# Two-layer macaron block on one core: routing taken further ahead, three PSUM banks in turn for the experts, and the second call's row scatters in twos

## What is computed

```python
x = x + 0.5 * ffn(layernorm(x))          # call 0
x = x + attn(layernorm(x))               # state-space mixer, then a gated FFN
x = x + 0.5 * ffn(layernorm(x))          # call 1

def ffn(x):
    shared = (silu(x @ sw1) * (x @ sw2)) @ sw3
    probs = softmax(x @ rw + rb)                 # 8 experts
    w, idx = top_k(probs, 2); w = w / sum(w)
    routed = sum over the two chosen e of w_e * ((silu(x @ ew1[e]) * (x @ ew2[e])) @ ew3[e])
    return shared + routed
```

## Time and profile before

| | us |
|---|---|
| median of 3 timed runs | 864.18 (860.76 to 873.64) |
| profiled execution | 854.65 |
| its span, first to last instruction | 852.9 |
| PE busy in the span | 658.5 |
| DVE busy | 546.5 |
| POOL busy | 518.7 |
| ACT busy | 413.9 |

### The profile page before, as it was taken

One profiled execution on the slowest core, in us unless ns is written; L12 is line 12 of the kernel. 1 busy time (PEld: TensorE's weight loads), 2 busy tenths in 40 slices (PEclk: granted clock), 3 DMA queues, 4 the chain that ended last, 5 costly groups with the idle time before them and its releaser, 6 DMA issues.

```text
span 852.9 us, 13745 instructions
## 1 busy us (share of the span) xinstructions
PE 658.5 (77%) x3768; PEld 479.3 (56%) x3768; DVE 546.5 (64%) x1730; ACT 413.9 (49%) x713; POOL 518.7 (61%) x656
## 2 busy tenths in 40 slices
PE   2548389888870557989999998989774989889940
PEld 2325257777760225656676765757552568777730
DVE  5545355544545787897999999997452545554528
ACT  1212124444430899997999998652121234444310
POOL 3875573555564675896978879767736305555550
PEclk9987789999995859889999998999978899999975
DMA  9311123222215100000000000000101123222218
GB/s 268 129 50 37 41 70 73 77 75 74 70 43 158 40 0 1 1 2 1 1 2 1 2 14 13 14 19 24 41 14 45 50 45 81 73 73 75 63 46 271
DMA packets 55512, 46.34 MB, mean 54 GB/s; under 512 B 8456, under 2 KB 51053, under 8 KB 55440
## 3 DMA queue, kind: packets, MB, share of 16 engines
q1 hardware_dynamic: 46736, 28.54, 12.6%
q0 software_dynamic: 8704, 16.93, 6.1%
HBM read 25.30 MB, written 21.19 MB: 55 GB/s over the span
## 4 chain that ended last, share of the span: by engine, by line
PE 47%; DVE 15%; issue 12%; another core or an unknown queue 11%; ACT 9%; POOL 3%; DMA 2%; DVEq 0%; POOLq 0%; ACTq 0%; SPq 0%
PE ps_go L2029 5%; PE ps_tr L1631 3%; PE ps_a L1971 3%; PE ps_b L1973 3%; PE ps_go L1981 3%; PE ps_go L1631 2%; DVE x L1516 2%; PE ps_go L1802 2%; PE ps_tr L1819 2%; PE ps_go L1806 2%; PE ps_b L1853 2%; PE ps_go L2018 2%; PE ps_go L1852 2%; POOL ys L710 1%
## 5 line engine op out<-in xcount | busy, mean ns | idle before, releaser
L710 POOL DMA_INDIRECT ys<-arena,dest x144 | 140.9, 978 | 145.1 <-DVE arena L1508 60.3
L694 POOL DMA_INDIRECT xs<-rows,pos x128 | 126.0, 985 | 72.8 <-DVE pos L1428 36.6
L2029 PE MATMUL ps_go<-w_down_e,arena 128*128 x576 | 80.0, 282 | 17.7 <-DVE arena L1508 15.7
L2029 PEld LDWEIGHTS ps_go<-w_down_e,arena 128*128 128x128 f32 x576 | 71.0, 194 | 24.0 <-issue 23.7
L1508 DVE COPY arena<-ps_go 128x256 f32<-128x256 f32 x72 | 30.6, 424 | 63.7 <-remote 40.5
L992 ACT ACTIVATE silu_a<-ps_a 128x512 f32<-128x512 f32 x32 | 19.1, 596 | 87.8 <-PE ps_a L1971 42.6
L1004 ACT ACTIVATE xt_hi<-ps_tr 128x256 fp32r<-128x256 f32 x72 | 27.4, 384 | 67.4 <-PE ps_tr L1992 42.5
L1021 ACT ACTIVATE arena<-ps_go 128x512 f32<-128x512 f32 x72 | 43.1, 598 | 28.5 <-remote 14.3
L1498 DVE TENSOR_TENSOR hid<-silu_a,ps_a 128x512 f32<-128x512 f32 x36 | 24.7, 687 | 41.1 <-ACT silu_a L1012 29.4
L2018 PE MATMUL ps_go<-ident,hid 128*128 128x128 f32 x288 | 44.0, 276 | 5.2 <-ACT arena L1021 5.1
L2018 PEld LDWEIGHTS ps_go<-ident,hid 128*128 128x128 f32 x288 | 35.1, 142 | 17.6 <-issue 7.7
(11 more groups left out here) (359 smaller groups left out, 1996.8 us busy)
## 6 DMA issues: line engine op xcount, KB each, us to landing
arena<-xs SPq DMA_DIRECT2D x144, 65.0 KB
rows<-ys SPq DMA_DIRECT2D x8, 512.0 KB, 4.2
arena<-ys SPq DMA_DIRECT2D x8, 512.0 KB, 7.5
ys<-arena,dest POOLq DMA_INDIRECT x144
x<-in_L_attn_x SPq DMA_DIRECT2D x8, 256.0 KB, 4.5
arena<-in_L_ffn_ew SPq DMA_DIRECT2D x4, 512.0 KB, 6.4
xs<-rows,pos POOLq DMA_INDIRECT x128
out<-x SPq DMA_DIRECT2D x8, 256.0 KB, 4.1
```

The lines of the kernel that those rows point to most:

```text
L694: pool.indirect_dma_start(xs, bass.IndirectOffsetOnAxis(pos[:, n, i:i + 1], 0), rows[:, n * TT + i % TT, :], None).then_inc(scattered, 16)
L710: pool.indirect_dma_start(ys, bass.IndirectOffsetOnAxis(dest[:, i:i + 1], 0), y_out[:, p % YRING, j, :], None, bounds_check=2 * TOK - 1, o ...
L2029: r = pe.matmul(ps_k[:, j * P:(j + 1) * P], hid_t[:, p % 2, at:at + P], w_down_e[:, bass.ds(which[2 * p + j], 1), k, :].rearrange("p a d - ...
```

## The change

Four edits. In call 0 the queues of PE, ScalarE and VectorE are written in another order, so that logits and choices are made two blocks ahead of the shared FFN and the ranks come first in each step. In call 1 the late blocks' routing is spread over more steps, and stands later in the queues. In the experts stage of both calls the banks `ps_k`, `ps_t` and `ps_r` are used in turn for transposes and answers; the wait for an answer's copy stands at the transposes now (`pe_tiles_t`), from the sixth pair on. In call 1, those of the mixer included, each pair of scatters waits until all scatters ahead of it have landed.

```diff
+        ps_turn = (ps_k, ps_t, ps_r)
+        def ps_tiles(p):
+            return ps_turn[(2 * p + 1) % 3][:, 0:2 * P]
+        def ps_answers(p):
+            return ps_turn[(2 * p + 2) % 3][:, 0:2 * P]
...
             pool.wait_ge(pos_ready, turn + 1)
             for i in which:
+                if turn >= NB and i % 2 == 0:
+                    pool.wait_ge(scattered, 16 * (turn * 2 * TT + i))
                 pool.indirect_dma_start(xs, bass.IndirectOffsetOnAxis(pos[:, n, i:i + 1], 0),
...
         def pe_tiles_t(pe, call, p):
             pair = call * NPAIR + p
-            after(pe, lo_ready, pair - 1)
+            if p >= 5:
+                pe.wait_ge(answer_ready, pair - 4)
...
-                r = pe.transpose(ps_tr[:, p % 2, j * P:(j + 1) * P], x_tiles[:, i % XIN, 0:P], ident[:, :])
+                r = pe.transpose(ps_tiles(p)[:, j * P:(j + 1) * P], x_tiles[:, i % XIN, 0:P], ident[:, :])
...
             pe.wait_ge(ht_ready, pair + 1)
-            after(pe, answer_ready, pair)
+            if p + 2 >= NPAIR:
+                pe.wait_ge(answer_ready, pair - 2)
...
             for n in range(1, NB + 2):
+                if n + 1 < NB:
+                    dve_places(dve, own, n + 1)
+                if n + 3 < NB:
+                    dve_norm(dve, n + 3)
                 if n + 2 < NB:
-                    dve_norm(dve, n + 2)
-                if n + 1 < NB:
-                    dve_route(dve, own, n + 1)
+                    dve_route(dve, own, n + 2)
                 if n <= NB:
                     dve_hid(dve, n - 1, 0)
-                if n + 1 < NB:
-                    dve_places(dve, own, n + 1)
-                if n + 2 == NB:
+                    dve_hid(dve, n - 1, 1)
+                if n + 1 == NB:
                     dve_tiles(dve, own, 0)
-                if n <= NB:
-                    dve_hid(dve, n - 1, 1)
...
             for n in range(NB + 1):
-                late = EARLY + n
+                late = EARLY + n - 1
                 if n < NB:
                     pe_up(pe, NB + n, 0)
-                if late < NB:
+                if EARLY <= late - 2 < NB:
+                    pe.wait_ge(rank_read, NB + late - 2)
+                    pe_rank(pe, NB + late - 2)
+                if EARLY <= late - 1 < NB:
+                    pe.wait_ge(logits_read, NB + late - 1)
+                    pe_route_logits(pe, late - 1, ps_r)
+                if n < NB:
+                    pe_up(pe, NB + n, 1)
+                if EARLY <= late < NB:
                     pe.wait_ge(xt_ready, NB + n + 2)
                     pe_route_xt(pe, late, ps_t)
...
```

More of the change, by code:

```diff
@@ L1025, in act_ffn @@
             act_xt(act, 1)
+            act_xt(act, 2)
             act.wait_ge(shared_in, 48)
@@ L1547, in dve_ffn @@
             dve_norm(dve, 2)
+            dve_norm(dve, 3)
+            dve_route(dve, own, 2)
             dve_w_lo(dve, 0)
             for n in range(1, NB + 2):
+                if n + 1 < NB:
+                    dve_places(dve, own, n + 1)
+                if n + 3 < NB:
+                    dve_norm(dve, n + 3)
                 if n + 2 < NB:
-                    dve_norm(dve, n + 2)
-                if n + 1 < NB:
-                    dve_route(dve, own, n + 1)
+                    dve_route(dve, own, n + 2)
                 if n <= NB:
                     dve_hid(dve, n - 1, 0)
-                if n + 1 < NB:
-                    dve_places(dve, own, n + 1)
-                if n + 2 == NB:
+                    dve_hid(dve, n - 1, 1)
+                if n + 1 == NB:
                     dve_tiles(dve, own, 0)
-                if n <= NB:
-                    dve_hid(dve, n - 1, 1)
                 if n >= 2:
@@ L1571, in dve_ffn_again @@
             dve.wait_ge(mixer_done, NB)
-            late = range(EARLY, NB)
-            for n in late:
+            for n in range(EARLY, NB):
                 dve_stats(dve, own, NB + n)
-            for n in late:
-                dve_norm(dve, NB + n)
             for n in range(NB + 1):
+                late = EARLY + n - 1
                 if n < NB:
                     dve_hid(dve, NB + n, 0)
-                if 1 <= n <= NB - EARLY:
-                    dve_places(dve, own, NB + EARLY + n - 1)
+                if EARLY <= late - 2 < NB:
+                    dve_places(dve, own, NB + late - 2)
+                if EARLY <= late - 1 < NB:
+                    dve_route(dve, own, NB + late - 1)
                 if n < NB:
                     dve_hid(dve, NB + n, 1)
+                if n == 0:
+                    for m in range(EARLY, NB):
+                        dve_norm(dve, NB + m)
                 if n:
                     dve_shared(dve, NB + n - 1)
-                if n < NB - EARLY:
-                    dve_route(dve, own, NB + EARLY + n)
-                if n == NB - EARLY:
+                if late - 2 == NB - 1:
                     dve_tiles(dve, own, 1)
@@ L2040, in pe_ffn @@
             pe_rank(pe, 0)
+            pe_logits(pe, 1)
             for n in range(NB + 1):
                 if n + 1 < NB:
-                    pe_logits(pe, n + 1)
+                    pe.wait_ge(rank_read, n + 1)
+                    pe_rank(pe, n + 1)
+                if n == 0:
+                    pe_xt(pe, 2)
+                if n + 2 < NB:
+                    pe_logits(pe, n + 2)
                 if n == 1:
@@ L2059, in pe_ffn @@
                     pe_down(pe, n - 2)
+                if n + 3 < NB:
+                    pe_xt(pe, n + 3)
             pe_down(pe, NB - 1)
@@ L2069, in pe_ffn_again @@
             for n in range(NB + 1):
-                late = EARLY + n
+                late = EARLY + n - 1
                 if n < NB:
                     pe_up(pe, NB + n, 0)
-                if late < NB:
+                if EARLY <= late - 2 < NB:
+                    pe.wait_ge(rank_read, NB + late - 2)
+                    pe_rank(pe, NB + late - 2)
+                if EARLY <= late - 1 < NB:
+                    pe.wait_ge(logits_read, NB + late - 1)
[3 more added lines that the diff above has]
+                if EARLY <= late < NB:
                     pe.wait_ge(xt_ready, NB + n + 2)
                     pe_route_xt(pe, late, ps_t)
-                if 0 <= n - 1 < NB - EARLY:
-                    pe.wait_ge(rank_read, NB + late - 1)
-                    pe_rank(pe, NB + late - 1)
-                if n < NB:
-                    pe_up(pe, NB + n, 1)
-                if late < NB:
-                    pe.wait_ge(logits_read, NB + late)
-                    pe_route_logits(pe, late, ps_r)
+                if n:
+                    pe_down(pe, NB + n - 1)
                 if n + 2 < NB:
-                    if late < NB:
+                    if EARLY <= late < NB:
                         pe.wait_ge(rx_ready, late + 1)
                     pe_xt(pe, NB + n + 2)
-                if n:
-                    pe_down(pe, NB + n - 1)
             pe_experts(pe, 1)
```

22 lines of the change are left out of this document (7 added, 15 removed).

## The result

The changed kernel takes 868.91 us (median of 20 runs, 865.32 to 872.89) and the kernel before 860.87 (20 runs, 857.62 to 873.64): a ratio of 1.0092, 95% interval 1.0074 to 1.011. That is 8 us slower where I forecast 16.5 us faster. The profiled execution took 869.42 us, its span 867.4 (854.65 and 852.9 before).

A forecast was written before the change was run, and what follows sets the result against it. It took PE to lead the chain (47%), with 11% from signals held under POOL's scatter trains. First call -6, second call -2.5 and experts -8 sum to -16.5 us from 864.2: 848 us, range 828 to 870.

The forecast's parts named there:

- PE's signals are held under a train of scatters: Mixer's end, shared FFN, experts: three or more close scatters hold PE's done signals until the last lands; two do no harm.
- the train of pairs becomes what the loads wait for: Second call: twelve late pairs end at 686.6, tile loads start about 686.8 instead of 690.31, PE idle before.
- the experts' cycle: Experts, both calls: POOL's scatters, landing, held signal and VectorE's copy set a cycle of 7.0 us for two pairs.
- Second call, -2.5 predicted: Mixer's end to experts' start, late routing with paired scatters: net -2.5 us, bounds -7 and +7.
- Break-even: Second call: the experts' start neither gains nor loses at 3.87 us per pair of scatters.
- my 3.65: Second call: assumed us per scatter pair with its wait, within 3.4 to 4.5, from a landing of 2.15.
- The low bound: Scatter landing in the second call: at least about 1.9 us after its start, when its packets end; high bound 3.05.
- Rival C: Second call: scatters land 3.05 us after starting, a pair takes 4.5; +11 instead of -2.5, total 861; chance 0.08.
- First call, -6 predicted: First call, routing two blocks ahead: less PE waiting, 12.9 us, against 7 us of longer holds; bounds -13 and +16.
- Rival E: First call: an unbroken scatter train holds PE's signals almost throughout; +16 for -6, total 870; chance 0.12.
- Experts, -8 predicted: Experts, both calls, three banks in turn: -8 us, about halfway to -14; bounds 0 and -38 (every pair at 2.94).
- Rival D: Experts: the banks give nothing because the cycle belongs to POOL; total 856; chance 0.16.

The follow-up runs named there:

- before_again: The kernel before, unchanged, as a run of its own on a chip with held signals: ratio 0.9999.
- the rstd ahead: Changed kernel with the fifth block's last three scatter pairs moved behind POOL's three late rstd, all pair waits kept: 0.9996 of the kernel before.
- number 6: Kernel before with one call's new routing order alone: first call's 1.01 with held signals, 1.001 and 1.0005 without; second call's 1.0018 without.

## Why the prediction was wrong

**What held.** The reading that PE's signals are held under a train of scatters and not under pairs: no "remote" is left where the pairs are, and the mixer's last addition follows its product. That the train of pairs becomes what the loads wait for, with PE idle ahead of it (19.06 us) and then at the lower clock, was right as well, and so was the experts' cycle (from one scatter after VectorE's answer to the next such, 726.83 to 733.89 is 7.06 us after, 7.0 before).

**Second call, -2.5 predicted, +10.8 in the trace.** This is the step that failed, and by more than its bounds (-7 to +7). The -2.5 was counted to the experts' start, with the lower clock in it; at the first down product it is +10.6, so the two ends agree. The loads came at 705.16 for 686.8. A late pair took 4.00 us, not 3.65: 11 x 0.35 = 3.9. The other 14.4 are the first late scatter, 657.4 for 643. Of them 11.2 are the rstd, which I had for 631.8: the mixer's train started at 614.72 and not near 606, since the pairs ahead of it pushed POOL's last additions of the mixer back (613.28; 603.43 before, 4 of the 10 us from the first call), and its pairs took 4.38 each. I had given those blocks 2 us to spare and priced the wait only at the end. The remaining 3 are the FFN restarting behind the rstd: PE had waited 7.46 us, and three steps at the lower clock took 2.4 us more than at full clock (1.08, 3.62 and 0.87 us for 0.60, 1.95 and 0.60). With the rstd ahead, the first late scatter stands at 645.13, which is near the 643 that I had summed up: what was wrong was the place of the rstd, and the rest of that sum held. Break-even was named rightly as 3.87 us a pair; my 3.65 was a choice near the packets' end, between bounds of 3.4 and 4.5 that held the truth. The low bound was itself misread: by rows 6 the packets end at 620.6, 1.7 us after the scatter's start, and no row gives the 620.74 that I wrote. The Trainium skill, "Perfetto Trace Analysis", in what it says of a semaphore that follows the last write's confirmation, was the better guide: 1.6 to 2.2 us pass from the end of the second scatter's record to the wait's end. Rival C, given 0.08, has the mechanism, with a pair between mine and its 4.5.

**First call, -6 predicted, +5.0 in the trace.** I wrote of the tile table that it is "made one block later" with "cover enough, and 2 us late at worst". I looked at the pads and the loads, not at what POOL does beside it. The memsets that the table had missed by some 5 us in the trace of before now hold it for 6.36. The gain didn't come either: I had POOL waiting less for positions and scattering in one long train, and it waits 15.5 us in four breaks, where it was 14.9 in three. Alone, the order cost 1.0% on the one chip with held signals where it ran, and nothing where none are; that it gains nothing there either says that ranks and choices were not what set the loads' start. Rival E's mechanism, longer holds, shows, though not at its size: the longest of the first call are 9.2 us on VectorE and 12.3 on ScalarE, and were 7.0 and 10.3.

**Experts, -8 predicted, about 0.** PE is 0.9 and 3.2 us quicker in the two calls, POOL's last scatter 0.3 in the second. Rival D (0.16) was right: the cycle is POOL's. I had put it in the text and still taken the middle. The far bound of -38 was wrong as well: the 236.5 us from first to last down product in both calls, less 70 pairs of 2.94, are -31.

**Sum.** The parts in the trace: +5.0 to the first down product, -0.9 to the last, +10.8 to the second loads, -0.3 from these to the last scatter; 14.6 in sum, and the spans differ by 14.5. The medians differ by 8. The profiled execution of before was faster than all its timed runs; my sum started from the median, which was sound. Against the kernel before's other trace on such a chip (before_again) the same parts are +5.4 and +8.8 instead of +5.0 and +10.8: a part read from two single traces is uncertain by 2 us, and in the first call by more (number 6).

**Open.** Whether it is the shared port by which memsets hold up VectorE; why the parts don't add up where signals are held; why some chips hold signals and others don't; what the table's 5 us are worth at the end; and the worth of the second call's order where signals are held, which was not run alone there.

## What to carry over

A wait put into an engine's queue costs first what stands behind it there: write down the next instruction of another kind (here three short rstd), and who waits for it, before pricing the wait itself. When a step moves to another time, look at what every engine that shares a port with it does at the new time. And measure a stage to the engine that ends it: PE was 3 us quicker in the second call's experts and the stage was not.

## What was not expected of the hardware

- The same kernel takes 782 us on two of the chips and 855 to 861 on the others. The clock is not most of it: the kernel before was granted 0.92 to 0.93 on those at 782 us and 0.90 to 0.91 on those at 855, and 0.02 more of 0.905 on PE's 658.5 us is, as an estimate, 15 of the 73 us at most. With held signals 167.5 us of waits are put down to "remote", without them none. A change made to avoid held signals costs 1.0339 where there are none and 1.0092 where there are.
- A 128x72 TENSOR_SCALAR of VectorE, 0.20 us, takes 6.36 to 6.41 us when it meets eleven memsets of POOL in a row, and a 128x8 cast 2.16 and 3.49; each ends at the first gap between POOL's instructions, of 0.12 us or so.
- In the changed kernel's trains of pairs the wait for a scatter's landing ends 2.5 to 3.2 us after the start of its record (0.96 and then 1.6 to 2.2); in the trace of before, a scatter's packets had ended 1.7 us after the start. A pair takes 4.0 to 4.4 us so, where it took 2.53.
